# A gated two-layer network with experts on one core: the orders of three engines and the PSUM banks laid out anew

## Chip, core, metric

The kernel runs on one core of a Trainium2 chip. The metric is device microseconds of one execution, as the median of several runs.

## What is computed

The input is x, 4 x 256 tokens of 256 numbers (1024 tokens), and a context of the same shape. Four gated residual steps follow one another:

```python
x = x + tanh(g_xattn[0]) * wkv(w, u, layernorm(x), ctx)      # a scan along the sequence, exp and running max
x = x + tanh(g_ffn[0])   * quantised_ffn(layernorm(x))       # ternary weights, 8-bit rows, silu(gate) * up, 1024 inner
x = x + tanh(g_xattn[1]) * cross_attention(layernorm(x), ctx) # 32 heads of 8; q and k rms-normed; softmax
x = x + tanh(g_ffn[1])   * moe(layernorm(x))                 # 64 experts of 64 inner, top 8 of the logits, a shared one
```

In the quantised step a weight becomes round(w / mean|w|) cut to -1, 0, 1, and a row of tokens round(x / s) with s = max|x| / 127. In the expert step every expert is computed for all tokens, and its inner rows are multiplied by the token's routing weight, which is zero for experts that were not chosen:

```python
gu = einsum('nh,eih->nei', x, gu_w); inter = silu(gu[..., :I]) * gu[..., I:]
out = einsum('nei,ehi->nh', inter * W[:, :, None], dp_w) + sigmoid(x @ g1.T) * shared(x)
```

## The kernel before

The kernel is written in raw instructions: five engines with a program each, semaphores between them, and the order of the work written out by hand. TensorE (PE) has the matrix products and transposes, VectorE (DVE) and ScalarE (ACT) share the elementwise work and empty PSUM, SyncE (SP) issues all the DMAs. Each engine's program is a list of calls of small functions, and the three lists are meant to match: `turn_norm(q, b0)` on PE transposes the rows of the q-th layernorm into bank b0, `high_halves(q, b0)` on ACT and `low_halves(q, b0)` on DVE read them there. Where a name has two arguments, the last is the PSUM bank (of eight). A bank is taken by PE only when its former reader is done, so bank numbers set waits too.

The 1024 tokens are eight tiles of 128, in two halves of 512. Products that need more than 16-bit precision are made of a high and a low f16 part (three products for one). Twelve norms in all (`NORM_TILES`, L290) are computed in an order given by the list `FORMER`; `stats(q)` gathers mean and variance, `norm(q)` (L986 to L989, L1028) waits for ACT's root (`norm_root`, L564, L566), and from norm 8 on the root is made on DVE itself.

There are three parts.

The front (to the first expert product): the scan, the quantised step for tokens of the first half, attention for that half (`scores`, ACT's `probabilities`, `weighted_values`, DVE's `heads_sum` and `heads_out`), the router's `logits` (L1690), and the first expert weights. For the quantised step ACT scales each of the three weights to integers (`to_integers`, L584) and cuts one from below (`clamp_from_below`, L590), DVE makes them ternary (`ternary_weights`, L1109, L1110, L1113); ACT scales the tokens' rows (`tokens_to_integers`, L667); PE multiplies (`gate_product`, `up_product`, four matmuls of 128x512 a tile, L1602); ACT takes the SiLU of the gate's (`ffn_silu`, L688), and DVE multiplies by the up product (`ffn_inner`, L1206). `project` and `turn_rows` prepare keys and queries (ACT evicts them at L629, L632, L634), `row_sums` and `rows` rms-norm them on DVE (three Newton steps of three instructions each for 64 numbers, L1000 to L1002, among them).

The first half's experts: 65 chunks follow one another. Chunks 0 to 31 are the 32 pairs of experts for the first 512 tokens, chunk 32 the shared expert, chunks 33 to 64 the pairs for the second half. A chunk is, on PE, two products into PSUM (gate and up; `experts_in`, L1562, six matmuls each) and, two chunks later, one out of the inner rows into the accumulators in banks 0, 1, 4 and 5 (`experts_out`, L1892, six matmuls); on ACT the SiLU (`experts_silu`, L931 to L934) and a high part (`experts_high`, L941); on DVE the product with the up half (L1478, L1481), the low part (`experts_low`, L1472) and the routing weight (L1491, L1494). The weights of a pair come from memory in f32 into one of two staging slots (`load_entry`, L499 to L510) and are split by ACT (`weights_high`, L732) and DVE (`weights_low`, L1277) into one of nine weight slots; SP issues the load of the next entry only when both halves of the last but one are done. Entries are numbered by pair.

Beside chunks 0 to 27 runs the second half's share of all the rest: its quantised step (in halves of a tile, `wide_products`, `wide_silu`, `wide_inner`), its norms 8 to 11, its attention and its logits. Three tables say what stands where: `BESIDE_SCALAR` (L319), `BESIDE_VECTOR` and `BESIDE_PRODUCTS`, by chunk and place. PE's loop is: first product of chunk c, what stands at (c, "A"), second product, (c, "B"), the output of chunk c - 2, (c, "C"). DVE's is: product of c, A, low part of c - 1, B, weighting of c, C. ACT's is: SiLU of c, A, high part of c - 1, B. The gate and up products have one pair of banks in the first half, and `gate_bank` gives a second pair only after the shared chunk. From chunk 28 on nothing but experts is left on PE.

Of the kernel before, what the change touches and what calls it, by code (L numbers as in the profile page):

```python
# [16 lines left out]
B, S, D = 4, 256, 256  # L17
# [29 lines left out]
def bass_flamingo(nc, x_in, ctxT_in, wkv_in, g_in, ffn_in, proj_in, gate_in, gu_in, dp_in,  # L47
                  identf_in, identh_in, routing, out):
    with ExitStack() as stack:
# [260 lines left out]
        def of_keys(n):  # L310
# [10 lines left out]
                ("turned_rows", 9, 7), ("wide_silu", 5, 1, 4)],  # L321
            (1, "A"): [("ffn_turned", 4, 6), ("ffn_scale", 5), ("wide_silu", 6, 0, 6), ("wide_silu", 6, 1, 4)],
            (2, "A"): [("weights_high", 5), ("ffn_turned", 5, 6), ("ffn_scale", 6), ("wide_silu", 7, 0, 6),
                ("weights_high", 6), ("wide_silu", 7, 1, 4)],
            (3, "A"): [("weights_high", 7), ("ffn_turned", 6, 4), ("ffn_scale", 7)],
            (4, "A"): [("ffn_turned", 7, 4)],
            (4, "B"): [("high_halves", 8, 4), ("weights_high", 8)],
            (5, "B"): [("project", 10, 7), ("project", 11, 6), ("weights_high", 9), ("project", 12, 7),
                ("project", 13, 6), ("weights_high", 10)],
            (6, "B"): [("split", 10), ("split", 11), ("high_halves", 9, 4)],  # L330
            (7, "B"): [("project", 14, 7), ("project", 15, 6)],
            (8, "A"): [("weights_high", 11)],
            (9, "A"): [("turned_rows", 10, 7), ("turned_rows", 11, 6), ("weights_high", 12)],
            (9, "B"): [("split", 12), ("split", 13)],
            (10, "A"): [("weights_high", 13)],
            (10, "B"): [("table_exp_tanh",), ("probabilities", 32, 4), ("probabilities", 33, 6)],
            (11, "A"): [("probabilities", 34, 4), ("probabilities", 35, 6)],
            (11, "B"): [("weights_high", 14), ("turned_rows", 12, 4), ("turned_rows", 13, 6)],
            (12, "A"): [("probabilities", 36, 4)],
            (12, "B"): [("probabilities", 37, 6), ("probabilities", 38, 4), ("weights_high", 15),  # L340
                ("probabilities", 39, 6)],
            (13, "B"): [("weights_high", 16), ("probabilities", 40, 4), ("split", 14), ("probabilities", 41, 6)],
            (14, "A"): [("probabilities", 42, 4)],
            (14, "B"): [("weights_high", 17), ("probabilities", 43, 4), ("probabilities", 44, 6),
                ("weights_high", 18), ("probabilities", 45, 4)],
            (15, "B"): [("split", 15), ("weights_high", 19), ("probabilities", 46, 6), ("weights_high", 20)],
            (16, "A"): [("probabilities", 47, 6), ("turned_rows", 14, 5)],
            (16, "B"): [("weights_high", 21), ("turned_rows", 15, 6), ("weights_high", 22)],
            (17, "B"): [("weights_high", 23), ("probabilities", 48, 4), ("probabilities", 49, 6)],
            (18, "A"): [("probabilities", 50, 4), ("probabilities", 51, 6)],  # L350
            (18, "B"): [("weights_high", 24), ("probabilities", 52, 4)],
            (19, "A"): [("probabilities", 53, 6)],
            (19, "B"): [("probabilities", 54, 4), ("probabilities", 55, 6)],
            (20, "A"): [("weights_high", 25)],
            (20, "B"): [("probabilities", 56, 4), ("probabilities", 57, 6), ("probabilities", 58, 4),
                ("probabilities", 59, 6)],
            (21, "A"): [("weights_high", 26)],
            (21, "B"): [("probabilities", 60, 4), ("weights_high", 27), ("probabilities", 61, 6),
                ("probabilities", 62, 4)],
            (22, "B"): [("probabilities", 63, 4), ("table_silu",), ("high_halves", 10, 6), ("weights_high", 28),  # L360
                ("weights_high", 29)],
            (24, "A"): [("high_halves", 11, 4)],
            (25, "B"): [("table_exp_tanh",), ("weights_high", 30), ("exp_logits", 1), ("weights_high", 31)],
            (26, "A"): [("table_silu",)],
            (26, "B"): [("turned_weights", 1, 7)],
            (27, "B"): [("weights_high", 32)],
# [3 lines left out]
            (1, "A"): [("wide_inner", 6, 0, 7), ("wide_inner", 6, 1, 5)],  # L370
            (1, "B"): [("ffn_residual", 4, 4)],
            (2, "A"): [("weights_low", 5), ("wide_inner", 7, 0, 7), ("wide_inner", 7, 1, 5)],
            (2, "B"): [("ffn_residual", 5, 6), ("stats", 8)],
            (3, "A"): [("norm", 8)],
            (3, "C"): [("ffn_residual", 6, 7), ("weights_low", 6)],
            (4, "C"): [("ffn_residual", 7, 7), ("stats", 9), ("low_halves", 8, 4), ("weights_low", 7),
# [170 lines left out]
        def _(act):  # L547
# [21 lines left out]
            def norm_root(q):  # L569
                first_root(NORM_TILES[q][1] - NORM_TILES[q][0])  # L570
# [1404 lines left out]
```

## Time and profile before

| | us |
|---|---|
| runs | 498.81, 496.13, 495.12 |
| median | 496.13 |
| the profiled execution's own time | 494.66 |
| its span in the profile | 492.9 |
| its mean granted clock of PE | 0.946 |

The span runs from the first to the last instruction that the profile shows, and is 1.8 us shorter than the execution's own time. All that the prediction works out is read from this one execution, in microseconds from the start of its span. L562 and such are lines of the kernel before.

### The profile page before, as it was taken

What the parts mean: (1) busy time and instruction counts of PE and PEld (TensorE: products, weight loads), DVE (VectorE), ACT (ScalarE), POOL (GpSimd) and SP (SyncE); (2) the same over time, 40 slices, a digit from 0 to 9 for tenths busy, and PEclk for the clock granted to TensorE, in tenths of its full rate; (3) what the DMA queues carried; (4) which work ended last, traced back from release to release, by engine and by line L of the source; (5) the groups of instructions that cost most, each with busy time, mean ns of one, the idle gap of its engine ahead of it and who ended that gap; (6) DMA issues with size and microseconds to landing.
All of it is one profiled execution on the core that took longest, in us unless ns stands there. A gap on an engine that the chain in (4) does not pass through costs nothing.

```text
span 492.9 us, 7899 instructions
## 1 busy us (share of the span) xinstructions
PE 401.6 (81%) x2606; PEld 191.7 (39%) x2606; DVE 384.4 (78%) x867; ACT 305.9 (62%) x473; POOL 0.2 (0%) x4
## 2 busy tenths in 40 slices
PE   1041765777774999989999899899999999999994
PEld 1020353332332555444334433444444444444442
DVE  5999489898999789999878876886546776677744
ACT  5989576689893785648887678463233445544431
POOL 0000000000000000000000000000000000000000
PEclk9996889595998799999999999999999999999999
DMA  8420000000020151525246332234421755555501
GB/s 306 198 65 1 0 1 1 1 1 2 1 65 4 47 165 57 158 88 168 67 118 191 98 108 72 91 108 125 132 65 54 217 164 164 164 177 172 171 22 43
DMA packets 31491, 47.47 MB, mean 96 GB/s; under 512 B 5594, under 2 KB 15194, under 8 KB 30940
## 3 DMA queue, kind: packets, MB, share of 16 engines
q1 hardware_dynamic: 31452, 46.98, 30.4%
q8 instruction: 21, 0.34, 0.3%
q14 instruction: 18, 0.15, 0.1%
HBM read 45.65 MB, written 1.31 MB: 95 GB/s over the span
## 4 chain that ended last, share of the span: by engine, by line
PE 47%; DVE 30%; ACT 8%; issue 7%; DMA 5%; SPq 2%; DVEq 0%; ACTq 0%
PE ps L1562 25%; PE ps L1892 12%; PE ps L1667 4%; DMA regP<-in_dp_dram 4%; PE ps L1655 2%; DVE regW L1277 2%; DVE bn L1009 1%; DVE tiny L1194 1%; ACT regO L584 1%; DVE xn L1028 1%; DVE regW L1481 1%; DVE regW L1472 1%; PE ps L1583 1%; DVE rep L1155 1%; DMA regC<-in_ctxT_dram 1%
## 5 line engine op out<-in xcount | busy, mean ns | idle before, releaser
L1562 PE MATMUL ps<-hH,regC 128*128 128x512 f16 x264 | 85.5, 379 | 1.1 <-ACT regW L934 0.9
L1481 DVE TENSOR_TENSOR regW<-ps,regW 128x512 f32<-128x512 f32 x65 | 44.9, 690 | 52.6 <-PE ps L1562 50.1
L934 ACT ACTIVATE regW<-ps 128x512 f32<-128x512 f32 x52 | 31.0, 596 | 86.6 <-PE ps L1562 83.5
L1562 PE MATMUL ps<-hH,regW 128*128 128x512 f16 x248 | 81.8, 386 | 1.4 <-ACT regW L934 0.8
L1562 PE MATMUL ps<-hL,regC 128*128 128x512 f16 x132 | 50.0, 379 | 0.0
L1892 PE MATMUL ps<-regW,regC 128*128 128x512 f16 x198 | 48.2, 379 | 0.5 <-DVE regW L1472 0.5
L1562 PE MATMUL ps<-hL,regW 128*128 128x512 f16 x124 | 47.8, 385 | 0.0
L1892 PE MATMUL ps<-regW 128*128 128x512 f16 x186 | 45.3, 380 | 0.7 <-DVE regW L1472 0.7
L1472 DVE TENSOR_TENSOR regW<-regW 128x512 f16<-128x512 f32 x65 | 44.4, 682 | 1.0 <-ACT regW L941 0.7
L941 ACT CAST regW<-regW 128x512 f16<-128x512 f32 x65 | 39.8, 612 | 6.4 <-DVE regW L1494 6.1
L1562 PEld LDWEIGHTS ps<-hH,regC 128*128 128x128 f16 x264 | 25.8, 98 | 33.3 <-issue 2.6
L723 ACT ACTIVATE exs<-ps 128x1024 f32<-128x1024 f32 x32 | 32.0, 1023 | 9.4 <-PE ps L1655 8.6
L1562 PEld LDWEIGHTS ps<-hH,regW 128*128 128x128 f16 x248 | 24.5, 99 | 33.0 <-issue 3.9
L1494 DVE TENSOR_TENSOR regW<-regW 128x512 f32<-128x512 f32 x52 | 35.6, 685 | 0.1
L723 ACT ACTIVATE regF<-ps 128x1024 f32<-128x1024 f32 x32 | 32.0, 1026 | 5.0 <-PE ps L1667 2.2
L732 ACT ACTIVATE regC<-regP 128x768 f16<-128x768 f32 x30 | 25.3, 844 | 15.7 <-DMA regP<-in_dp_dram 15.7
L1277 DVE SCALAR_TENSOR_TENSOR regC<-regP,regC 128x768 f16<-128x768 f32 x30 | 28.5, 953 | 8.1 <-ACT regC L732 8.0
L1554 PE MATMUL ps<-identf,xn 128*128 128x128 f32 x64 | 12.6, 341 | 26.4 <-DVE xn L1028 15.8
L1655 PE MATMUL ps<-regO,KT 32*128 32x256 f16 x256 | 21.8, 290 | 9.4 <-ACT exs L723 3.8
L1892 PEld LDWEIGHTS ps<-regW,regC 128*128 128x128 f16 x198 | 19.1, 98 | 24.1 <-DVE regW L1472 1.0
L732 ACT ACTIVATE regW<-regP 128x768 f16<-128x768 f32 x27 | 22.6, 844 | 8.8 <-DMA regP<-in_dp_dram 8.5
L1277 DVE SCALAR_TENSOR_TENSOR regW<-regP,regW 128x768 f16<-128x768 f32 x27 | 25.5, 952 | 2.9 <-ACT regW L732 2.9
(189 smaller groups left out, 657.1 us busy)
## 6 DMA issues: line engine op xcount, KB each, us to landing
regW<-routing_dram SPq DMA_DIRECT2D x130, 128.0 KB, 3.1
regP<-in_gu_dram SPq DMA_DIRECT2D x56, 256.0 KB, 2.7
regP<-in_dp_dram SPq DMA_DIRECT2D x56, 128.0 KB, 2.8
regO<-in_ffn_dram SPq DMA_DIRECT2D x3, 1024.0 KB, 9.0
x<-in_x_dram SPq DMA_DIRECT2D x2, 512.0 KB, 8.2
regC<-in_ctxT_dram SPq DMA_DIRECT2D x1, 1024.0 KB, 5.0
out_dram<-x SPq DMA_DIRECT2D x2, 512.0 KB, 3.3
regP<-in_proj_dram SPq DMA_DIRECT2D x1, 768.0 KB, 12.1
```

The lines of the kernel that those rows point to most:

```text
L723: nc.scalar.activation(Ex[u % NE], bank(b0, 2).rearrange("p (j n) -> p j n", j=2), ACT.Exp, scale=float(HD) ** -0.5).then_inc(prob_ready, 1)
L732: nc.scalar.activation(mwH[e % NW], mst[:, e % NS, :], ACT.Copy, scale=W_SCALE).then_inc(mwH_ready, 1)
L934: nc.scalar.activation(sgm[:, c % 2, :], bank(gate_bank(c)), ACT.Silu, scale=UNSCALE).then_inc(esilu_done, 1)
L941: nc.scalar.copy(inH[:, d % 2, :], inter[:, d % 2, :]).then_inc(inH_ready, 1)
L1277: V.scalar_tensor_tensor(mwL[e % NW], mst[:, e % NS, :], W_SCALE, mwH[e % NW], ALU.mult, ALU.subtract).then_inc(mwL_ready, 1)
L1472: V.tensor_tensor(inL[:, d % 2, :], inter[:, d % 2, :], inH[:, d % 2, :], ALU.subtract).then_inc(inL_ready, 1)
L1481: V.tensor_tensor(rows, bank(gate_bank(c) + 1), rows, ALU.mult).then_inc(et_done, 1)
L1494: V.tensor_tensor(rows, route[:, c % NR, :], sgm[:, c % 2, :], ALU.mult).then_inc(inter_ready, 1)
L1562: mm = T.matmul(out_ap, w(k), a(k), start=(n == 0), stop=(n == 3 * DK - 1))
L1655: mm = T.matmul(bank(b0 + jj)[:, mt * S:(mt + 1) * S], KT[r:r + 32, g, b * S + mt * P:b * S + (mt + 1) * P], QT[r:r + 32, g, (b % 2) * S:( ...
L1667: mm = T.matmul(bank(bk)[32 * j:32 * j + HD + 1, 0:S], vaug[:, 2 * b + mt, 4 * g + j, :], Ex[u % NE][:, j % 2, mt * S:(mt + 1) * S], start ...
L1892: mm = T.matmul(bank(ACC[h] + k), w[s][:, at], a[:, c % 2, :], start=(c == 0 and n == 0), stop=(c == NCH - 1 and n == 2), skip_group_check ...
```

## The change

Each engine's list of calls is put in another order, and PSUM's bank numbers with it. It touches the lists of the front on ACT, DVE and PE, and the three tables beside the first half's experts. Each engine makes the same calls with the same shapes as before; SP's order, the chunks and their loop, the buffers, and all from chunk 28 on stay. The diff is cut to the lines that the prediction speaks of; of a table one or two lines stand. The functions' bodies are nine lines higher up in the kernel after (L1562 before is L1553 after).

```diff
         BESIDE_SCALAR = {
...
-            (4, "B"): [("high_halves", 8, 4), ("weights_high", 8)],
...
+            (5, "A"): [("high_halves", 8, 6)],
...
         BESIDE_VECTOR = {
...
-            (5, "C"): [("row_sums", 10), ("row_sums", 11), ("rows", 5), ("norm", 9)],
...
+            (12, "C"): [("norm", 9)],
+            (13, "C"): [("low_halves", 9, 6), ("heads_sum", 18, 5), ("weights_low", 19), ("heads_sum", 19, 4),
+                ("rows", 6)],
...
         BESIDE_PRODUCTS = {
...
-            (1, "A"): [("turn_rows", 9, 7), ("wide_products", 5, 1, 4)],
+            (1, "A"): [("wide_products", 5, 1, 4), ("turn_rows", 9, 7)],
...
-            (25, "A"): [("logits", 1, 7)],
```

DVE's list in the front, its beginning and its end:

```diff
             sums_a(0)
             sums_b(0)
+            sums_c(0)
             sums_a(1)
             sums_b(1)
-            sums_c(0)
+            sums_c(1)
             low_part(1)
             low_part(2)
-            sums_c(1)
+            weight_scales()
             quotient(0)
             quotient(1)
-            weight_scales()
-            row_sums(0)
+            ternary_weights(0)
             add_y(0, 4)
             stats(1)
-            ternary_weights(0)
+            ternary_weights(1)
+            row_sums(0)
+            row_sums(1)
+            ternary_weights(2)
             norm(1)
             token_scales(0)
-            ternary_weights(1)
-            ternary_weights(2)
-            ffn_inner(0, 4)
+            ffn_inner(0, 6)
...
+            weights_low(4)
             norm(7)
-            weights_low(2)
-            weights_low(3)
             low_halves(7, 2)
             logits(0, 1)
-            weights_low(4)
```

PE's list in the front, its beginning:

```diff
             turn_norm(0, 4)
-            project(0, 7)
-            project(1, 6)
             sum_weights()
+            project(0, 6)
+            project(1, 7)
             turn_y(0, 4)
-            turn_norm(1, 6)
-            up_product(0, 4)
-            gate_product(0, 6)
+            turn_norm(1, 2)
+            gate_product(0, 4)
+            up_product(0, 6)
             gate_product(1, 2)
```

In the tables these calls move too. The weights' entries 13, 14, 15, 16, 17, 19, 30, 31 and 32 are split on DVE at (10, "A"), 11C, 12C, 13B, 14C, 15B, 26B, 26C and 27C before, and at 8C, 9B, 10B, 11C, 11C, 13C, 25A, 26A and 27A now. `turn_rows(9)` changes places with the wide product beside it in 1A; norm 9, its low halves, `project(14)` and `project(15)`, two `rows` and `ffn_residual(7)` move from chunks 4 to 10 to chunks 11 to 16; norm 10 moves from 18A to 17C and norm 11 from 22C to 23C; the second half's logits move on PE from 25A to 25C.

The first place is ACT between the scan's exponentials and the quantised products, before norm 1's root (L564, L566 before, L555, L557 after). Before:

```order
L629 ACTIVATE kc<-ps 128x256
L632 ACTIVATE sq<-ps 128x256
L634 ACTIVATE vaug<-ps 128x32x8
L629 ACTIVATE kc<-ps 128x256
L632 ACTIVATE sq<-ps 128x256
L634 ACTIVATE vaug<-ps 128x32x8
L584 ACTIVATE regO<-regO,magic,rws 128x2048 x3
L564 ACTIVATE lnv<-ve 128x4
L566 ACTIVATE root<-lnv 128x4
L758 ACT_TABLE_LOAD
L590 ACTIVATE fw<-regO,magic 128x2048
```

After:

```order
L575 ACTIVATE regO<-regO,magic,rws 128x2048
L620 ACTIVATE kc<-ps 128x256
L623 ACTIVATE sq<-ps 128x256
L625 ACTIVATE vaug<-ps 128x32x8
L575 ACTIVATE regO<-regO,magic,rws 128x2048
L620 ACTIVATE kc<-ps 128x256
L623 ACTIVATE sq<-ps 128x256
L625 ACTIVATE vaug<-ps 128x32x8
L581 ACTIVATE fw<-regO,magic 128x2048
L575 ACTIVATE regO<-regO,magic,rws 128x2048
L555 ACTIVATE lnv<-ve 128x4
L557 ACTIVATE root<-lnv 128x4
```

The three scalings of weights (regO) stand apart now, with the evictions of two projections (kc, sq, vaug) between them, and the clamp (fw) stands ahead of the root instead of behind it.

The second place is DVE at the end of the front, from the last norm's statistics (bn, mv) to the logits (regF, 128x4x65). Before:

```order
L1009 BN_STATS bn<-x 128x6 x2
L1012 BN_AGGR mv<-bn 128x2 x2
L977 TENSOR_SCALAR ve<-mv 128x2
L986 TENSOR_TENSOR newt<-ve,root 128x2
L987 TENSOR_TENSOR newt<-newt,root 128x2
L988 TENSOR_SCALAR newt<-newt 128x2
L989 TENSOR_TENSOR rstd<-newt,root 128x2
L1028 TENSOR_SCALAR xn<-x,mv,rstd 128x256 x2
L1277 SCALAR_TENSOR_TENSOR regW<-regP,regW 128x768 x2
L1170 TENSOR_TENSOR hL<-ps,hH 128x256 x2
L1250 TENSOR_SCALAR regF<-ps 128x4x65
```

After:

```order
L1000 BN_STATS bn<-x 128x6 x2
L1003 BN_AGGR mv<-bn 128x2 x2
L968 TENSOR_SCALAR ve<-mv 128x2
L1268 SCALAR_TENSOR_TENSOR regC<-regP,regC 128x768
L977 TENSOR_TENSOR newt<-ve,root 128x2
L978 TENSOR_TENSOR newt<-newt,root 128x2
L979 TENSOR_SCALAR newt<-newt 128x2
L980 TENSOR_TENSOR rstd<-newt,root 128x2
L1019 TENSOR_SCALAR xn<-x,mv,rstd 128x256 x2
L1161 TENSOR_TENSOR hL<-ps,hH 128x256 x2
L1241 TENSOR_SCALAR regF<-ps 128x4x65
```

The two low splits of expert weights (regW) between the norm's rows (xn) and the low halves (hL) are gone from here, and another one (regC) stands between the statistics and the root's steps.

The third place is PE where the rows of norm 9 are turned (L1554 before, in chunk 6; L1545 after, in chunk 13). Before:

```order
L1892 MATMUL ps<-regW,regC 128x512 x6
L1554 MATMUL ps<-identf,xn 128x128 x4
L1562 MATMUL ps<-hH,regC 128x512
L1562 MATMUL ps<-hL,regC 128x512
L1562 MATMUL ps<-hH,regC 128x512 x2
L1562 MATMUL ps<-hL,regC 128x512
L1562 MATMUL ps<-hH,regC 128x512 x2
L1562 MATMUL ps<-hL,regC 128x512
```

After:

```order
L1883 MATMUL ps<-regW 128x512 x6
L1545 MATMUL ps<-identf,xn 128x128 x4
L1658 MATMUL ps<-exs,vaug 9x256 x8
L1658 MATMUL ps<-regF,vaug 9x256 x8
L1553 MATMUL ps<-projH,hH 128x256
L1553 MATMUL ps<-projL,hH 128x256
L1553 MATMUL ps<-projH,hL 128x256
L1553 MATMUL ps<-projH,hH 128x256
```

Before, the next expert product (hH, hL) stood behind the turned rows; now two weighted values (exs and regF with vaug) and then the projection of these very rows (projH, projL) stand there.

## Rows read from the trace of the kernel before

**Rows 1.** The page's busy time, share of the span and instructions of each engine.

```profile
PE 401.6 (81%) x2606; PEld 191.7 (39%) x2606; DVE 384.4 (78%) x867; ACT 305.9 (62%) x473; POOL 0.2 (0%) x4
```

**Rows 2.** Stretches: length, busy PE, PEld, DVE, ACT, POOL (instructions), PE's clock, DMA share, GB/s.

```profile
0.00:162.34 162.34, 85.91 (x743) 46.33 (x744) 139.11 (x355) 120.74 (x187) 0.20 (x4) 0.86 0.14 51
162.34:230.43 68.09, 64.39 (x367) 33.71 (x364) 62.72 (x170) 47.64 (x81) 0.00 (x0) 0.97 0.36 107
230.43:277.24 46.81, 45.44 (x368) 19.15 (x367) 37.61 (x71) 38.16 (x49) 0.00 (x0) 1.00 0.42 127
277.24:341.31 64.07, 60.48 (x443) 26.61 (x441) 49.20 (x128) 38.88 (x58) 0.00 (x0) 1.00 0.32 100
```

**Rows 3.** Chain of waits from 341.31 us: start, us, what.

```profile
345.37 2.59 PE ps L1562 x12
347.96 1.29 PE ps L1892 x6
```

**Rows 4.** DVE's waits, 56 to 162 us: for whom, us in total, times, longest.

```profile
DVE regF L1206 <- ACT regF L688: 6.1, 1, 6.1
DVE regO L1163 <- PE ps L1583: 1.1, 3, 0.7
DVE newt L986 <- ACT root L566: 1.1, 2, 0.6
```

**Rows 5.** PE's waits in the first half's experts, 162.4 to 341.4 us.

```profile
PE ps L1554 <- DVE xn L1028: 1.9, 2, 1.5
PE ps L1562 <- ACT regW L934: 1.7, 2, 0.9
PE ps L1655 <- DVE x L1243: 1.4, 2, 1.0
PE ps L1644 <- DVE x L1226: 1.0, 1, 1.0
PE ps L1562 <- DVE regW L1481: 0.7, 2, 0.6
```

**Rows 6.** ACT's timeline, 33 to 50 us: start, us, instruction [idle before, releaser].

```profile
33.36 0.39 ACT L629 ACTIVATE kc<-ps 128x256 f32<-128x256 f32 x1 [0.64 <-PE ps L1562]
...
36.35 6.06 ACT L584 ACTIVATE regO<-regO,magic,rws 128x2048 f32<-128x2048 f32 x3 [0.63 <-DVE rws L1103]
...
47.00 2.08 ACT L667 ACTIVATE xn<-xn,magic,rqs 128x256 f32<-128x256 f32 x4 [0.94 <-DVE rqs L1190]
```

**Rows 7.** DVE's timeline, 42 to 57 us.

```profile
42.85 0.16 DVE L986 TENSOR_TENSOR newt<-ve,root 128x4 f32<-128x4 f32 x1 [0.55 <-ACT root L566]
...
47.53 1.22 DVE L1109 TENSOR_SCALAR fw<-regO 128x2048 bf16<-128x2048 f32 x1
48.78 0.69 DVE L1110 TENSOR_SCALAR fw<-fw 128x2048 bf16<-128x2048 bf16 x1
55.62 1.28 DVE L1206 SCALAR_TENSOR_TENSOR regF<-ps,sus,regF 128x1024 f32<-128x1024 f32 x1 [6.14 <-ACT regF L688]
```

**Rows 8.** Chain of waits at the first quantised products.

```profile
51.22 3.22 PE ps L1602 x8
```

**Rows 9.** Two stretches around them, columns as in rows 2.

```profile
51.20:54.40 3.20, 3.18 (x9) 1.20 (x10) 0.00 (x0) 0.00 (x0) 0.00 (x0) 0.57 0.00 0
54.40:58.00 3.60, 3.48 (x17) 1.37 (x14) 2.35 (x2) 3.12 (x3) 0.00 (x0) 1.00 0.00 0
```

**Rows 10.** Timelines of DVE and ACT at the front's end.

```profile
157.97 1.82 DVE L1277 SCALAR_TENSOR_TENSOR regW<-regP,regW 128x768 f16<-128x768 f32 x2
...
159.01 0.65 ACT L661 CAST hH<-ps 128x256 f16<-128x256 f32 x2 [0.97 <-PE ps L1554]
```

**Rows 11.** DVE's groups by form, all the span: us busy, mean ns, idle before.

```profile
L1277 DVE SCALAR_TENSOR_TENSOR regC<-regP,regC 128x768 f16<-128x768 f32 x30 | 28.5, 953 | 8.1 <-ACT regC L732 8.0
...
L1000 DVE SCALAR_TENSOR_TENSOR newt<-rstd,ve 128x64 f32<-128x64 f32 x12 | 2.7, 225 | 0.4
```

**Rows 12.** Chain of waits from 296 us: a weight load behind its issue.

```profile
298.94 4.28 DMA regP<-in_dp_dram
```

More of the change, by code:

```diff
@@ new lines, in bass_flamingo @@
+            (3, "C"): [("narrow", 6, 5)],
+            (5, "A"): [("turn_norm", 8, 6)],
+            (5, "C"): [("turn_hidden", 7, 4), ("project", 10, 7), ("project", 11, 6)],
+            (6, "A"): [("project", 12, 7), ("project", 13, 6)],
+            (7, "B"): [("turn_rows", 10, 7)],
+            (8, "A"): [("turn_rows", 11, 7)],
+            (8, "C"): [("scores", 32, 4), ("scores", 33, 6)],
+            (11, "B"): [("scores", 34, 4)],
+            (12, "A"): [("scores", 35, 4), ("weighted_values", 16, 7), ("narrow", 7, 6)],
@@ L469, in bass_flamingo @@
+            (21, "B"): [("scores", 61, 4), ("scores", 62, 6)],
+            (21, "C"): [("scores", 63, 4)],
+            (22, "A"): [("weighted_values", 30, 7), ("weighted_values", 31, 6)],
+            (22, "B"): [("heads_out", 6, 4), ("heads_out", 7, 6)],
+            (25, "A"): [("turn_norm", 11, 4)],
+            (25, "C"): [("logits", 1, 7)],
+            (27, "B"): [("turn_weights", 1, 7)],
         }
@@ L1761, in _ @@
[L1761 to L1772 removed]
+            turn_hidden(2, 4)
+            narrow(2, 7)
+            turn_norm(2, 4)
+            turn_hidden(3, 2)
+            project(2, 6)
@@ new lines, in _ @@
+            project(3, 5)
+            project(4, 4)
+            narrow(3, 6)
+            project(5, 5)
+            turn_rows(0, 3)
+            turn_rows(1, 4)
+            turn_norm(3, 4)
+            turn_rows(2, 3)
+            turn_rows(3, 2)
+            scores(0, 0)
+            scores(1, 4)
+            scores(2, 6)
+            scores(3, 2)
+            scores(4, 0)
+            scores(5, 4)
+            weighted_values(0, 7)
+            scores(6, 2)
+            weighted_values(1, 6)
@@ new lines, in _ @@
+            turn_norm(4, 6)
+            scores(7, 0)
+            scores(8, 4)
+            weighted_values(2, 3)
+            weighted_values(3, 2)
+            scores(9, 0)
+            scores(10, 4)
+            scores(11, 6)
+            project(6, 3)
+            project(7, 1)
+            scores(12, 4)
+            weighted_values(4, 2)
+            weighted_values(5, 7)
+            turn_rows(4, 6)
+            turn_rows(5, 3)
+            scores(13, 0)
+            scores(14, 6)
+            scores(15, 4)
@@ L1798, in _ @@
-            scores(31, 4)
-            weighted_values(14, 2)
-            weighted_values(15, 3)
-            turn_norm(6, 4)
+            scores(20, 0)
+            scores(21, 6)
+            weighted_values(8, 3)
+            turn_y(1, 4)
+            weighted_values(9, 2)
+            turn_norm(5, 0)
+            weighted_values(10, 7)
+            scores(22, 4)
+            scores(23, 2)
+            scores(24, 6)
+            scores(25, 4)
+            scores(26, 2)
+            weighted_values(11, 1)
@@ L1802, in _ @@
+            scores(27, 6)
+            weighted_values(12, 5)
+            scores(28, 2)
+            scores(29, 6)
+            scores(30, 0)
+            weighted_values(13, 5)
+            scores(31, 2)
+            weighted_values(14, 4)
+            weighted_values(15, 7)
+            turn_norm(6, 5)
             heads_out(2, 2)
-            heads_out(3, 6)
+            heads_out(3, 0)
             wide_products(4, 0, 4)
```

550 lines of the change are left out of this document (234 added, 316 removed).

## The prediction

> **What bounds the kernel now.** I read the page's busy line first, then the busy times by stage, then each engine's waits inside a stage, and last the instructions around the waits. The busy line puts TensorE (PE) at 81% [rows 1]. That mean hides four stages [rows 2]. In the front (0 to 162.34 us, before the first expert product) VectorE (DVE) is busy 139.1 of 162.3 us and PE only 85.9: DVE bounds it. In the first half's experts PE is busy 64.39 + 45.44 + 60.48 = 170.3 of 179.0 us (chunks 0 to 10, 11 to 17, 18 to 28), while DVE is busy 92% of the first of these stretches (62.72 of 68.09) and 80% of the second. From 341.31 us on, the start of chunk 29, the chain of waits is a plain beat of PE: 2.59 us into an expert pair and 1.29 out of it, 3.88 us a chunk [rows 3]. The change leaves that part alone, so the question is how late PE arrives at it.
>
> What is there to win? In the front, after 56 us, DVE waits 6.1 us for the first SiLU, and the next largest group is 1.1 us [rows 4]. An order can't do away with work, so the front has few us to give. In the first half PE is idle 8.7 us, most of it behind DVE: 1.9 us for a norm's rows and 1.4 + 1.0 us for residuals, with 1.7 us for the experts' SiLU [rows 5]. The 8.7 us are the largest gain that the loop can have.
>
> **Part 1, the quantised products.** Before, ScalarE (ACT) runs the three scalings to integers in one piece (6.06 us from 36.35), 2.0 each, then the root for norm 1, then the clamp, as large as a scaling, beside DVE's norm [rows 6]. Now the scalings can start when the weight scales are there, after DVE's low parts (32.0, the 3.87 us of quotients no longer ahead), but two projections' evictions (three instructions of 0.39 us each [rows 6], 1.0 us a set) and the clamp stand before the root. 32.6 + 6.06 + 2 x 1.0 + 2.0 = 42.7: the root is as early as before (DVE took it up at 42.85 [rows 7]). DVE, though, now also has the last step of the second ternary weight (0.69), one row sum (0.4) and the third ternary weight (1.22 + 0.69 [rows 7]) ahead of norm 1; these lay in its 6.1 us gap. 3.0 us of work less the 0.6 us wait for the root [rows 4]: norm 1 begins near 45.4, and the tokens' integers at 49.5 instead of 47.00 [rows 6], 2.5 us later. Part comes back, since the gate product of tile 0 is now first and its SiLU runs beside the up product. 53.75 (51.22 + 2.5) + 3.22 for 8 products [rows 8] = 57.0, so `ffn_inner(0)` comes at 57.2 instead of 55.62 [rows 7]: + 1.6 us. Tile 1's up product is still the sixth call: 24 products, 3.22 + 16 x 0.205 (3.48 / 17 [rows 9]) = 6.5, and a bank's wait let it through near 61.0, where DVE is ready at 60.2: + 0.8. One row sum, and what followed it, is done already: - 0.6. Together + 1.8 us (bounds 0.5, if the clock is up when the burst starts, and 4.8, if it stays down throughout).
>
> The clock is the unsure part. From 51.2 to 54.4 us the granted clock was 0.57, so mostly the 1.2 GHz level, and 1.00 just after [rows 9]; my sum takes the first 8 products at that level again.
> The Trainium skill (TensorE: Matmul & The Clock Gate, What's actually happening) says that the throttled state is the default and activity releases it; by that the burst starts slow wherever it is put, and the sum stays + 1.8, or turns into rival C if release comes later. The trace agrees as to the start (0.57), and can't show the new place.
>
> **Part 2, the front's middle.** Between 67 and 90 us DVE's calls are mixed anew (row sums, residuals and turned rows stand behind one another), so the 1.1 us of waits for turned rows [rows 4] get other work beside them: - 0.9 us (bounds 0 and - 1.5).
>
> **Part 3, the front's end.** Before, two low splits of expert weights (1.82 us) filled the time between DVE's last norm and its low halves, while PE turned the rows and ACT made the high halves (begun 159.01, 0.65 us) [rows 10]. Now these two stand far earlier and a third (0.95 us [rows 11]) goes before the norm's roots. That one hides the 0.6 us wait for the root [rows 4] and costs some 0.4 us, and the low halves wait uncovered: the norm's rows end where the splits began, 157.97, and the high halves at 159.66, 1.6 us of nothing on DVE, while the two splits' 1.82 us now lie in busy time. 1.3 us of that shows before the first expert product, by my order of the calls ahead of it, and 0.4 + 1.3 less 0.4 for waits that the early splits fill is + 1.3 us (bounds 0 and 2.3). Front: 1.8 - 0.9 + 1.3 = + 2.2 us, so the first expert product starts near 164.5.
>
> **Part 4, chunks 0 to 10.** Counting calls in both orders, by chunk 10 DVE loses one statistics, one norm, two `rows` (each twelve chained steps at 0.225 us [rows 11], 2.7 us, and five more, some 3.8 by estimate), one low halves, two row sums, two low splits of rows and a residual, and gains two weight splits (0.95 each): about 14 us less. PE loses 2.7 us of work beside the experts. DVE held PE here, so its waits on a norm (1.9), on a residual (1.0) and on DVE's expert product (0.6) go [rows 5]; 1.0 us of new ones comes (`wide_products(5, 1)` stands ahead of the turned rows and waits for its bank, and `turn_norm(8)` is close behind its norm). - 2.7 - 3.5 + 1.0 = - 5.2, say - 5.0 us (bounds 0 and - 6.5).
>
> **Part 5, chunks 11 to 17.** The 14 us land here, and norm 10 (3.2 us) out of chunk 18. DVE's load is then 37.6 + 14 + 3.2 = 54.8 us, some 3 less where neighbouring instructions overlap; PE's is 45.4 + 2.7 = 48 in a stretch that took 46.8 [rows 2]. PE runs ahead of DVE by a chunk at most, since one pair of gate banks holds the products. Waits that I find one by one: 0.7 at the first scores behind their probabilities (chunk 12), 2.8 in chunk 13 (`turn_norm(9)` right behind norm 9; `project(14)` behind low halves 9), 1.4 in 15 and 16. Weights are a part of it: ACT waits for entry 19 before high halves 9, and a weight load took 4.28 us from issue to landing [rows 12]. Part 5: 2.7 + 4.9 - 1.4 (old waits of scores on a residual [rows 5]) = + 6.2 us (bounds + 2.7, if DVE's backlog hides in PE's lead, and + 12).
> The Trainium skill (DMA: Bandwidth & Descriptors, Anatomy of one DMA) gives, for the descriptor path of GpSimd, 2.0 us fixed and bytes at 436 GB/s: by it such a load of 128 KB would be an estimated 2.3 us and the sum 2 us less. Here the loads are on SyncE's hardware queue and share it, and the trace's 4.28 us [rows 12] decides.
>
> **Part 6, chunks 18 to 28.** Most of the old waits that lie here go, some 2.9 of the 8.7 us (entries 30 to 32 are split earlier). New: 1.2 in 18 and 19 (low halves 10 and heads' sums), 0.3 in 22, and 1.9 in 26, whose experts' product waits behind the logits, one place later. Together about - 0.6 us (bounds - 3 and + 3).
>
> **The sum.** 2.2 - 5.0 + 6.2 - 0.6 = + 2.8 us on the profiled execution's 494.66: 497.5. The median of the runs before (496.13) lies 1.5 us above that execution, so the forecast for a median is 498.9 us.
>
> **The rivals.** (A) The evening-out works. For it: DVE at 92% in one stretch and 80% in the next is uneven, the order moves 14 us across that line, and nearly all of PE's 8.7 us are behind something that an order can move. Against: the front. If all goes and nothing comes: 496.13 + 2.2 - 8.7 = 489.6. (B) Slower, by one mechanism: in chunks 11 to 17 DVE becomes the bound. It decides from the point where DVE's product of chunk 13 comes after PE has done both of that chunk's products. Then the stretch takes DVE's 54.8 us for PE's 46.8, + 8.0, and DVE, which is late, splits three entries late, each 1.3 us more: + 12.0 in place of + 6.2, so 504.7. For it: the sum of loads. Against: neighbouring DVE instructions overlap. (C) PE's clock: the burst's 24 products all run at 0.40 us, 9.6 us in place of 6.5, + 3.0: 501.9.
>
> **How the numbers follow.** About 1% is what a measurement of this kernel tells from no change: 491.2 and 501.1. My forecast (496 to 501): 0.50. A: 0.18. B: 0.20. C: 0.12. So faster 0.18, same 0.50, slower 0.32. The range is 491.5 to 505.5: below it lies most of A, above it the worse half of B's tail, some 2 in 10 together.
>
> **What would show it.** The first expert product starts at 164 to 165 us; DVE's gap before `ffn_inner(0)` is 7 to 8 us instead of 6.1. PE's idle time up to chunk 10 is about 1 us. DVE is over 93% busy in chunks 11 to 17, and PE waits there for DVE. PE begins chunk 29 some 2 to 4 us later than 341.31. I am wrong if the first expert product starts before 162 us (parts 1 to 3), if PE is idle under 6 us over the first half (part 5), or if the beat from chunk 29 on isn't 3.88 us.

## The result, and the profile after

| | before | after |
|---|---|---|
| median of 20 runs, us | 495.54 | 498.46 |
| lowest to highest | 494.04 to 498.81 | 495.64 to 501.4 |
| profiled execution, us | 494.66 | 498.54 |
| its span | 492.9 | 496.8 |
| its mean granted clock of PE | 0.946 | 0.938 |

The ratio of after to before is 1.0047, with a 95% interval of 1.003 to 1.0064: slower by 1.5 to 3.2 us, real, and inside the 1% that the prediction called no change. The quotient of the two medians is 1.0059; here and below it lies inside the interval, up to 0.0024 from the ratio. The forecast was 498.9.

The stretches of the kernel after, cut at the same places of the program as in [rows 2] (first expert product, start of chunk 11, of chunk 18, of chunk 29), with the same columns:

```profile
0.00:164.45 164.45, 90.44 (x743) 48.12 (x743) 139.58 (x356) 121.18 (x187) 0.20 (x4) 0.84 0.14 51
164.45:230.18 65.73, 61.84 (x342) 32.27 (x340) 53.93 (x133) 43.59 (x71) 0.00 (x0) 0.96 0.39 121
230.18:282.11 51.93, 47.64 (x391) 21.57 (x390) 46.51 (x112) 38.59 (x54) 0.00 (x0) 1.00 0.31 94
282.11:345.22 63.11, 60.04 (x447) 26.86 (x444) 49.76 (x126) 41.86 (x61) 0.00 (x0) 1.00 0.37 114
```

The lengths against [rows 2] are + 2.11, - 2.36, + 5.12 and - 0.96 us, + 3.91 in all, and the executions' own times differ by 3.88. From chunk 29 on the beat is the same 3.88 us.

DVE's timeline in the front answers to [rows 7]:

```profile
45.22 0.16 DVE L977 TENSOR_TENSOR newt<-ve,root 128x4 f32<-128x4 f32 x1
...
57.14 1.28 DVE L1197 SCALAR_TENSOR_TENSOR regF<-ps,sus,regF 128x1024 f32<-128x1024 f32 x1 [7.81 <-PE ps L1593]
...
60.59 1.28 DVE L1197 SCALAR_TENSOR_TENSOR regF<-ps,sus,exs 128x1024 f32<-128x1024 f32 x1 [0.47 <-PE ps L1593]
...
161.82 0.76 DVE L1161 TENSOR_TENSOR hL<-ps,hH 128x256 f16<-128x256 f32 x2 [1.41 <-ACT hH L652]
```

Norm 1's root steps begin at 45.22 instead of 42.85, `ffn_inner(0)` comes 1.52 us later than before, and the low halves at the front's end stand uncovered for 1.41 us. PE's waits answer to [rows 5]. From the first expert product to chunk 11:

```profile
PE ps L1593 <- ACT regF L703: 2.1, 1, 2.1
PE ps L1690 <- DVE Wf L1262: 1.0, 1, 1.0
PE ps L1646 <- ACT regO L645: 0.6, 1, 0.6
```

And in chunks 11 to 17:

```profile
PE ps L1553 <- DVE hL L1161: 1.4, 1, 1.4
PE ps L1646 <- ACT exs L714: 1.2, 1, 1.2
PE ps L1658 <- ACT regF L714: 0.7, 1, 0.7
PE ps L1646 <- ACT regF L714: 0.5, 1, 0.5
PE ps L1553 <- DVE regW L1472: 0.4, 1, 0.4
```

None of the old waits of the first group is left (a norm's rows, a residual, DVE's product). Others of the same size stand in their place, and most name ACT, not DVE. The largest, 2.1 us, is a wide product that waits for a bank which `ffn_turned(5)` (L703) frees. A wait of the same kind was in this stretch before, with 0.6 us (L712 and L1602 before are L703 and L1593 after):

```profile
PE ps L1602 <- ACT regF L712: 0.6, 1, 0.6
```

The chain of waits in chunks 2 and 3 tells what held ACT:

```profile
178.01 0.60 SPq L531
...
178.71 0.53 SPq L500
...
179.28 4.41 DMA regP<-in_dp_dram
...
184.46 1.10 ACT regF L703
...
185.70 1.19 PE ps L1593 x4
```

and ACT's timeline shows it standing:

```profile
180.61 0.85 ACT L723 ACTIVATE regC<-regP 128x768 f16<-128x768 f32 x1
183.71 0.84 ACT L723 ACTIVATE regC<-regP 128x768 f16<-128x768 f32 x1 [2.25 <-DMA regP<-in_dp_dram]
184.46 1.10 ACT L703 ACTIVATE regF<-ps,magic 128x1024 bf16<-128x1024 f32 x1
```

ACT's list now has the split of entry 6 (the second L723) right ahead of `ffn_turned(5)`. The entry's load is issued at 178.71, behind SyncE's route loads, and lands 4.4 us later. ACT takes its list in order, so the tile behind the split waits for a load that it doesn't need. Before, this split came after three other calls and waited for nothing:

```profile
182.38 0.83 ACT L732 ACTIVATE regC<-regP 128x768 f16<-128x768 f32 x1
```

Two further places look alike: a split of entry 12 ahead of `turned_rows(11)` (ACT waits 2.12 us, PE 0.6), and one of entry 19 ahead of `high_halves(9)` (ACT waits 1.29 us, DVE 0.47 for those high halves, and PE 1.4 for the low ones).

### The profile page after: what moved, and what is told of

Same layout as the page of the kernel before. It is cut to its first block, busy times and chain, and to the rows that moved or that the text cites. A ratio compares the mean times of both kernels' runs of the same rounds, so it can differ in the third digit from the quotient of the medians.

```text
span 496.8 us, 7898 instructions
## 1 busy us (share of the span) xinstructions
PE 405.3 (82%) x2606; PEld 194.7 (39%) x2606; DVE 384.2 (77%) x867; ACT 305.3 (61%) x473; POOL 0.2 (0%) x4
## 4 chain that ended last, share of the span: by engine, by line
PE 46%; DVE 32%; issue 7%; DMA 6%; ACT 5%; SPq 4%; DVEq 0%; ACTq 0%
PE ps L1553 25%; PE ps L1883 12%; DMA regP<-in_dp_dram 5%; SPq L531 2%; PE ps L1658 2%; DVE bn L1000 2%; PE ps L1593 2%; DVE xn L1019 1%; DVE regO L1226 1%; PE ps L1646 1%; DVE regW L1463 1%; DVE regW L1268 1%; DMA regC<-in_ctxT_dram 1%; DVE regW L1485 1%; DVE tiny L1185 1%
## 5 line engine op out<-in xcount | busy, mean ns | idle before, releaser
L1553 PE MATMUL ps<-hH,regC 128*128 128x512 f16 x264 | 85.5, 379 | 0.4 <-DVE regW L1472 0.4
L1553 PE MATMUL ps<-hH,regW 128*128 128x512 f16 x248 | 81.2, 384 | 1.2 <-DVE regW L1472 1.2
L1553 PE MATMUL ps<-hL,regC 128*128 128x512 f16 x132 | 50.0, 379 | 0.0
L1553 PE MATMUL ps<-hL,regW 128*128 128x512 f16 x124 | 47.5, 383 | 0.0
L1553 PEld LDWEIGHTS ps<-hH,regC 128*128 128x128 f16 x264 | 25.8, 98 | 32.2 <-issue 2.1
L1545 PE MATMUL ps<-identf,xn 128*128 128x128 f32 x64 | 13.4, 361 | 30.1 <-DVE xn L1019 14.0
L1553 PEld LDWEIGHTS ps<-hH,regW 128*128 128x128 f16 x248 | 24.6, 99 | 32.9 <-issue 3.4
L723 ACT ACTIVATE regC<-regP 128x768 f16<-128x768 f32 x30 | 25.3, 844 | 8.7 <-DMA regP<-in_dp_dram 8.2
L723 ACT ACTIVATE regW<-regP 128x768 f16<-128x768 f32 x27 | 22.7, 844 | 12.5 <-DMA regP<-in_dp_dram 12.3
```

Of the source, the lines that this page charges most:

```text
L723: nc.scalar.activation(mwH[e % NW], mst[:, e % NS, :], ACT.Copy, scale=W_SCALE).then_inc(mwH_ready, 1)
L1545: mm = T.transpose(bank(b0 + k)[:, (t - a) * P:(t - a + 1) * P], xn[:, t, k * P:(k + 1) * P], identf[:, :])
L1553: mm = T.matmul(out_ap, w(k), a(k), start=(n == 0), stop=(n == 3 * DK - 1))
```

## The experiments

In each run's text "after" is the changed kernel. Medians of different runs of the kernel before went from 495.5 to 497.0, so ratios are compared, and a difference in us is a difference of two ratios times the median of before. Positions come from one profiled execution each, and that one isn't always near the median of its run: e_norm's is the shortest of its twelve (495.00), e_end's the longest (497.99).

**The two halves of the change.** The run m_front has the new lists of the front with the old three tables, m_loop the reverse.

> The new order of the front alone, the first half's experts by the tables of before. Theory (the front costs about 2 us and the loop adds about 1 to 2): first expert product near 164.5 us, median 1.8 to 2.5 us over before (about 497.6). Rival (the front's delay is absorbed by waits in the loop, all of the loss is the loop's): first product late all the same, but the median within 0.7 us of before. A fault of the measurement (one execution was slow) would put the first product at 162 to 163.

Measured: median 499.45 beside 496.62, ratio 1.0033 (1.0006 to 1.0059): + 1.6 us. The first expert product is at 166.47, 2 us later than expected.

> The new tables beside the first half's experts alone, with the front of before. Theory (the loop's new order gives nothing: chunks 0 to 10 win 2.4 us, 11 to 17 lose 5.1, 18 to 28 win 1): median 0.5 to 2 us over before (about 496.5 to 497.5), first product at 162.3. Rival (the loop's order is better by itself and suffers only from a late start): median 1 us or more under before.

Measured: 497.05 beside 496.62, ratio 1.0005 (0.9977 to 1.0032): + 0.2 us. The first product came at 165.48 here, with the very front that gave 162.34 in the profile of before. Of these 3.14 us, 0.80 are there when PE turns norm 1's rows (48.54 instead of 47.74), 0.36 more at `ffn_inner(0)`, and 1.98 come between the fourth `ffn_inner` and the first product. PE's clock differs too. Its timeline at the quantised products, before and then in m_loop:

```profile
51.22 6.66 PE L1602 MATMUL ps<-fw,regF 128*128 128x512 bf16 x24 [1.40 <-issue]
```

```profile
48.54 2.08 PE L1545 MATMUL ps<-identf,xn 128*128 128x128 f32 x8 [11.27 <-ACT xn L658]
52.02 9.32 PE L1593 MATMUL ps<-fw,regF 128*128 128x512 bf16 x31 [1.40 <-issue]
```

At full clock such a product takes 0.222 us (28 in 6.21 us in e_warm below), so 24 would take 5.3 us and 31 would take 6.9: the low clock cost PE 1.3 us in one execution and 2.4 in the other. Behind the fourth `ffn_inner` the mean granted clock is 0.83 before and 0.81 here. That the clock makes all of the 3.14 us isn't shown.

Front alone and tables alone give + 1.6 and + 0.2, together + 1.8, and the whole change + 2.3 us (0.0047). By these ratios the loss is the front's, and the tables win and lose about the same; the two intervals overlap, so the profiles are asked too. Four have the old front (before, m_loop, e_oldfront, b_small), with the fourth `ffn_inner` at 64.67 to 66.27 us (mean 65.7) and the first product at 162.34 to 165.48 (163.4). Five have the new one unchanged (after, m_front, e_loads, e_first, e_small), at 66.63 to 68.50 (67.5) and 164.45 to 167.69 (166.0). The new front is late by 1.8 us at the first place and by 2.6 at the second.

**Norm 1 first.** In the kernel after:

```diff
             ternary_weights(0)
             add_y(0, 4)
             stats(1)
-            ternary_weights(1)
             row_sums(0)
-            row_sums(1)
-            ternary_weights(2)
             norm(1)
             token_scales(0)
+            ternary_weights(1)
+            row_sums(1)
+            ternary_weights(2)
```

> The kernel after, with one row sum, and the last two ternary steps behind DVE's norm 1 and token scales instead of ahead of them. Theory of part 1 (DVE's 3 us of work ahead of norm 1 make ffn_inner(0) late): norm 1 about 2.3 us earlier (limited by ACT's root, at 43.5), tokens' integers near 47.3, ffn_inner(0) near 55.0 instead of 57.14, first expert product near 162.5 and the median 1.5 to 2 us under the kernel after (about 496.7). Rival (the PE clock or the two ternary weights, now later, bound the products): ffn_inner(0) not before 56.5 and the median within 0.7 us of after.

Measured: 498.27, ratio 1.0022 (0.9993 to 1.0051), some 1.2 us under after's 1.0047, with overlapping intervals. DVE's timeline:

```profile
44.65 1.38 DVE L1019 TENSOR_SCALAR xn<-x,mv,rstd 128x256 f32<-128x256 f32 x4
...
55.91 1.28 DVE L1197 SCALAR_TENSOR_TENSOR regF<-ps,sus,regF 128x1024 f32<-128x1024 f32 x1 [5.10 <-PE ps L1593]
...
59.95 1.28 DVE L1197 SCALAR_TENSOR_TENSOR regF<-ps,sus,exs 128x1024 f32<-128x1024 f32 x1 [1.06 <-PE ps L1593]
```

Norm 1's rows begin 1.36 us earlier (44.65 instead of 46.01), not 2.3: ACT's root is the limit. `ffn_inner(0)` gains 1.23 us and the second tile 0.64: it waits 1.06 us for its products, 27 of which take 8.45 us here, most of it at the low clock. The mechanism is there, at half the size. What it is worth at the end is less sure: e_both below lies 1.6 us under e_loads, again with overlapping intervals.

**Splits of weights behind the urgent call.** In the kernel after, ACT's table:

```diff
-            (2, "A"): [("weights_high", 5), ("weights_high", 6), ("ffn_turned", 5, 4), ("ffn_scale", 6)],
+            (2, "A"): [("weights_high", 5), ("ffn_turned", 5, 4), ("ffn_scale", 6), ("weights_high", 6)],
-            (7, "B"): [("weights_high", 11), ("weights_high", 12), ("turned_rows", 11, 7)],
+            (7, "B"): [("weights_high", 11), ("turned_rows", 11, 7), ("weights_high", 12)],
-            (13, "B"): [("probabilities", 39, 4), ("weights_high", 19), ("high_halves", 9, 6), ("project", 14, 7),
+            (13, "B"): [("probabilities", 39, 4), ("high_halves", 9, 6), ("weights_high", 19), ("project", 14, 7),
```

> The kernel after, with three splits of expert weights on ACT (entries 6, 12, 19) put behind the call that PE waits for (ffn_turned 5, turned_rows 11, high_halves 9) instead of ahead of it. Theory W (ACT stands still before a split until its load lands, 2.25, 2.12 and 1.29 us, and PE waits 2.1, 0.6 and 1.4 us behind it): these three waits of PE go, PE's chunk 29 starts 2 to 4 us earlier than 345.22, median 495 to 496.5. Rival D (DVE is the bound in chunks 11 to 17, 46.5 of 51.9 us busy, and takes up what ACT gives back): the waits turn into waits on DVE, the median is within 1 us of the kernel after.

Measured: 495.19, ratio 0.9959 (0.9937 to 0.9982), clear of after's 1.0047 and 4.4 us under it. PE takes 175.2 us from the first expert product to chunk 29, 180.8 in after, so DVE doesn't take up what ACT gives back (theory W held, rival D didn't). The run e_first has the first of the three moves alone:

> The kernel after, with only one of the three moves of the run e_loads: the split of entry 6 on ACT stands behind ffn_scale 6 instead of ahead of ffn_turned 5 (chunk 2). Theory W1 (this one wait, 2.25 us on ACT and 2.1 on PE, makes most of the 3.3 us): the start of PE's chunk 3 is 2 us nearer to the first product than in the kernel after (20.7 to 21.9 us behind it in place of 23.95) and the median 2 us under after (about 496.5). Rival W3 (the gain came from the split of entry 19 in chunk 13, or from all three together): median less than 1 us under after.

Measured: 495.95, ratio 0.9984 (0.9954 to 1.0013), 3.1 us under after. The start of chunk 3 stands 20.74 us behind the first product in both, 23.95 in after, and 22.7 to 25.4 in the other runs with the split ahead: a wait for a load comes out differently each time. In e_first PE still waits 3.3 us in chunk 13, where the third move leaves 0.7 in e_loads:

```profile
PE ps L1553 <- DVE hL L1161: 3.3, 1, 3.3
```

W1 holds: the place of this one call is worth 3.1 us, clear of noise, more than the whole loss of 2.3. The 1.2 us from e_first to e_loads are inside the noise, and no run moves the splits of entries 12 and 19 one at a time; the waits point to entry 19.

**Smaller loads.** Each load from entry 5 on moves a quarter of its bytes; the rest of the expert weights in the slot is old data, so this part isn't computed from the inputs. The run e_small does this to the kernel after, b_small to the kernel before.

```diff
-                sp.dma_start(mst[:, e % NS, 0:2 * DK * P], gu_in[:, p, :]).then_inc(ld_pair[e % NS], 16)
-                sp.dma_start(mst[:, e % NS, 2 * DK * P:PW], dp_in[:, p, :]).then_inc(ld_pair[e % NS], 16)
+                w = 1 if e < NS + EARLY else 4
+                n1, n2 = 2 * DK * P // w, D // w
+                sp.dma_start(mst[:, e % NS, 0:n1], gu_in[:, p, 0:n1]).then_inc(ld_pair[e % NS], 16)
+                sp.dma_start(mst[:, e % NS, 2 * DK * P:2 * DK * P + n2], dp_in[:, p, 0:n2]).then_inc(ld_pair[e % NS], 16)
```

> The kernel after, with only a quarter of the bytes of each weight load from entry 5 on (64 KB and 32 KB in place of 256 and 128 KB; the rest of the staging slot keeps old numbers, so this part of the expert weights is not computed from the inputs). Theory W (bytes in flight make ACT stand before its splits): ACT's idle time before its splits of weights falls from 21 us to under 8, the start of chunk 3 comes 20.7 us behind the first product in place of 23.95, median 3 us under after. Rival F (what ACT waits for is mostly the late issue: SyncE's route loads and the splits that free a slot): the loads shorten by some 1 us each and ACT's idle time falls by less than half, median 0 to 1.5 us under after.

> The control to e_small: the kernel before, with a quarter of the bytes of each weight load from entry 5 on (that part of the expert weights is not computed from the inputs). In the kernel after this took 6 us off the median. If waits for loads are what the new order of the experts' part added, the kernel before gains clearly less, 1 to 3 us (median 493.5 to 495.5). If every order of this kernel pays for the loads alike, it gains 5 to 6 us too (median near 491), and the loads explain nothing of the difference between the two kernels.

Measured: e_small 492.34, ratio 0.9903 (0.9879 to 0.9927); b_small 493.53, ratio 0.9934 (0.9913 to 0.9955). The kernel after gains 7.1 us by ratio, twice what was expected; the kernel before 3.3, a little over its 1 to 3. Chunk 3 starts 20.76 us behind the first product, as theory W said. ACT's groups of splits, in after and then in e_small:

```profile
L723 ACT ACTIVATE regC<-regP 128x768 f16<-128x768 f32 x30 | 25.3, 844 | 8.7 <-DMA regP<-in_dp_dram 8.2
L723 ACT ACTIVATE regW<-regP 128x768 f16<-128x768 f32 x27 | 22.7, 844 | 12.5 <-DMA regP<-in_dp_dram 12.3 <-ACT vaug L625 0.2
```

```profile
L725 ACT ACTIVATE regC<-regP 128x768 f16<-128x768 f32 x30 | 25.4, 846 | 3.6 <-DMA regP<-in_dp_dram 3.6
L725 ACT ACTIVATE regW<-regP 128x768 f16<-128x768 f32 x27 | 22.7, 845 | 5.4 <-DMA regP<-in_dp_dram 4.9 <-ACT vaug L627 0.4
```

ACT's idle time falls from 21.2 to 9.0 us. In the kernel before it was 24.5 us, more than in after, and yet cost less: what counts is who is queued behind the split. With small loads after is faster than before (0.9903 against 0.9934, intervals that overlap) although its front still costs 1.6 us. The new tables were thus worth some 2 to 3 us where loads are short: 1.5 + 1.6 by the ratios, and 2.0 by the profiles, where the stretch from the first expert product to chunk 29 takes 173.6 us in e_small and 175.6 in b_small. The load waits ate that. That it comes from the evening-out of DVE, and not from another part of the new tables, is argued and not shown.

**PE's clock.** In the kernel after, 32 extra matmuls (128x512 into bank 0, never read) ahead of `turn_norm(1, 2)` on PE and 6 behind it.

```diff
+            def warm(n):
+                for _ in range(n):
+                    T.matmul(bank(0), projH[:, 0, 0:P], ctxH[:, 0, 0:512], start=True, stop=True)
...
+            warm(32)
             turn_norm(1, 2)
+            warm(6)
             gate_product(0, 4)
```

> The kernel after, with 32 extra matmuls (128x512, their result in bank 0 is never read) ahead of PE's transposes for norm 1 and 6 behind them. Theory C (the burst of quantised products starts at the 1.2 GHz level because PE was idle 12 us before it): with PE busy ahead of it the granted clock is 1.0 from the first product, 8 products take 1.7 us in place of 3.3, ffn_inner(0) comes at 55.3 or earlier instead of 57.14 and ffn_inner(1) without its 0.5 to 1 us wait, median 1.5 to 2.5 us under after. Rival (the level doesn't follow what PE did just before, or the extra activity lowers the clock later): products still at 0.4 us each, or a lower clock in the stretch behind them, and the median within 0.7 us of after or above.

The stretches of after around the products (its transposes begin at 50.02, its products at 53.59), then those of e_warm, and PE's timeline at e_warm's products:

```profile
50.00:53.50 3.50, 2.17 (x8) 1.15 (x8) 0.00 (x0) 2.71 (x5) 0.00 (x0) 0.50 0.00 0
53.50:57.00 3.50, 3.41 (x9) 1.26 (x10) 0.00 (x0) 1.11 (x1) 0.00 (x0) 0.54 0.00 0
```

```profile
40.00:50.00 10.00, 4.81 (x23) 2.07 (x22) 8.82 (x28) 5.42 (x7) 0.00 (x0) 0.99 0.00 1
50.00:53.50 3.50, 3.50 (x13) 1.85 (x14) 0.00 (x0) 2.58 (x5) 0.00 (x0) 0.53 0.00 0
53.50:57.00 3.50, 3.50 (x18) 1.60 (x17) 0.87 (x1) 1.46 (x2) 0.00 (x0) 1.00 0.00 0
```

```profile
53.86 6.21 PE L1593 MATMUL ps<-fw,regF 128*128 128x512 bf16 x28
```

The 32 matmuls ended 5.2 us ahead of the transposes. The transposes and the six extra matmuls ran at the low level (0.53), in the products' stead. From the first product on the granted clock is 1.00 instead of 0.54 (2.4 GHz in place of mostly 1.2), 18 matmuls fit where 9 did, and `ffn_inner(0)` comes at 56.13 instead of 57.14 (55.3 was expected). The median is 497.92, ratio 1.0018 (0.9997 to 1.0039), some 1.4 us under after with overlapping intervals. That the level follows what PE did just before is shown; the gain of the median alone would not have shown it.
The Trainium skill (TensorE: Matmul & The Clock Gate, What's actually happening) says that the throttled state is the default and that activity releases the throttle. The traces agree: each of the runs without extra matmuls starts this burst at the low level, and only e_warm and e_all don't.

**The front's end.** In the kernel after, the splits of entries 2 and 3 go back behind norm 7 and that of entry 4 behind the logits, on DVE and on ACT, as in the kernel before. DVE's part:

```diff
             heads_sum(14, 4)
-            weights_low(2)
             heads_sum(15, 7)
             split_low(8)
             split_low(9)
-            weights_low(3)
...
-            weights_low(4)
             norm(7)
+            weights_low(2)
+            weights_low(3)
             low_halves(7, 2)
             logits(0, 1)
+            weights_low(4)
```

> The kernel after, with the splits of entries 2, 3 and 4 on ACT and DVE back where the kernel before has them at the end of the front (2 and 3 behind the last norm's root and rows, 4 behind the logits). Theory of part 3 (their early place costs 1.3 us ahead of the first product): first expert product 1 to 1.5 us earlier than in after (near 163.2), median 1 us under after. Rival (the early splits also load entries 5 and 6 earlier, or the work has only changed places): first product within 0.5 us of 164.45 or the gain lost again by chunk 3, where entries 5 and 6 would land later; median within 0.7 us of after or above.

Measured: 495.35, ratio 0.9969 (0.9945 to 0.9994), 3.9 us under after. The profiled execution shows less. Its first product is at 164.67, but its burst had run at the low clock and the fourth `ffn_inner` started 0.91 us later than in after (67.54 against 66.63), so the rest of the front is 0.7 us shorter, and chunk 3 stands 23.05 us behind the first product, 0.9 less than in after. These 1.6 us are located. Beside the five profiles with the new front, where the fourth `ffn_inner` and the first product are 97.8 to 99.2 us apart (mean 98.5), e_end's 97.1 is 1.4 less, which is what was expected of it. The profiled execution is also the longest of the run's twelve. Where the rest of the runs' 3.9 us comes from is open.

**Both mended, and more.** The run e_both is the kernel after with the edits of e_norm and e_loads; e_oldfront is m_loop with those of e_loads; e_all is e_both with the extra matmuls of e_warm.

> The kernel after with both edits, norm 1 ahead of the ternary weights on DVE and the three splits behind the urgent calls on ACT. If the parts add: 3.3 us and 0.2 to 1.5 us under after, median 493.7 to 495. Rival (the front's gain is lost in the burst's clock, as in e_norm): median as in e_loads, 495.2 within 0.5.

> The front of the kernel before, with the new tables and the three moved splits of e_loads. If the front of after costs 1.6 to 2 us (m_front): median 493.2 to 494 and under both kernels. If the front costs nothing when the loop's loads are out of the way: median 495 as in e_loads.

> All that helped: the kernel after with norm 1 ahead of the ternary weights, the three splits behind the urgent calls, and the extra matmuls that keep PE's clock up. If the clock's 1 us at ffn_inner(0) is worth anything at the end: median 0.5 to 1 us under e_both (492.37), so 491.4 to 491.9. If it is lost again in the front's middle, as e_warm suggested: 492.4 within 0.5.

Measured: e_both 492.37, ratio 0.9926 (0.9897 to 0.9954), under the 493.7 to 495 expected; e_oldfront 492.99, 0.9917 (0.9888 to 0.9946), 2.1 us under e_loads, which is the front's cost once more (intervals that just overlap); e_all 490.59, 0.9872 (0.9842 to 0.9902). In e_both the parts add: 6.0 us under after, where e_norm and e_loads have 1.2 and 4.4. e_all is 2.7 us under e_both (intervals that just touch), more than either expectation and than e_warm's 1.4. e_all beats the kernel before by 6.3 us and the kernel after by 8.7. In its products' stretch the clock is full:

```profile
53.00:56.00 3.00, 3.00 (x16) 1.36 (x14) 1.30 (x2) 1.87 (x2) 0.00 (x0) 1.00 0.00 0
```

`ffn_inner(0)` stands at 54.67 there, and the first product at 160.66.

## Why the prediction came out right

The forecast was 498.9 and the median 498.46, and both profiled executions differ by 3.88 us where the sum said 2.8. Step by step:

- **Part 1 (+ 1.8) held.** Norm 1 at 45.22 (forecast 45.4), `ffn_inner(0)` at 57.14 (57.2), the fourth tile 1.96 us later than before. The nine profiles with an old or a new front give 1.8 us for this place in the mean, so this isn't one lucky trace, and e_norm confirms that the work ahead of norm 1 is a cause. The 0.205 us for a product at full clock was low, 0.222 by e_warm.
- **Parts 2 and 3 (- 0.9 and + 1.3) held in sum only.** From the fourth `ffn_inner` on the front lost another 0.15 us where 0.4 was forecast; in the mean of the nine profiles it loses 0.9. The waits for turned rows are gone and the low halves wait 1.41 us (1.6 forecast). The early splits cost 1.4 us ahead of the first product by e_end's profile (1.3 forecast for part 3), but more at the end by its ratio, which one trace doesn't explain. The first product's 164.45 beside the forecast 164.5 is partly luck, since it moves by some us from one execution to the next. The runs' value for the whole front is + 1.6 (m_front) to + 2.1 us (e_loads against e_oldfront); the forecast was + 2.2.
- **Part 4 (- 5.0) was too large: - 2.36.** The step that failed is "1.0 us of new ones comes". PE's idle time in chunks 0 to 10 is 65.73 - 61.84 = 3.9 us, against 3.7 before. I had counted the new waits by who stands behind whom on DVE and PE, and missed the split ahead of `ffn_turned(5)` on ACT. The waits that were to go were also read too large for this stretch: of the norm's 1.9 us, 1.5 lie here. With the split of entry 6 moved (e_first) the stretch takes 61.65 us, - 6.4.
- **Part 5 (+ 6.2) was near: + 5.12.** 2.2 us of it are PE's moved work (2.7 forecast), 2.9 idle time (3.5 net forecast). The wait in chunk 13 is there, 1.4 us in after and 3.3 in e_first; DVE stands for the high halves behind the load of entry 19 for 0.5 and 2.5 us of it. Two of its steps failed. DVE's load didn't rise by 17 us but by 8.9 (37.61 to 46.51). Overlap of rows explains little of that: the durations of the stretch add up to 40.3 us before and 50.3 after, + 10.0. Most of it is that I had moved calls by their place in the tables, while DVE runs behind PE's chunks. `rows(7)`, in chunk 10 of the old table, ran behind PE's start of chunk 11 (230.43) already before, and norm 10's root and rows, in chunk 17 of the new one, run behind its start of chunk 18 (282.11); the first instruction of each, before and then after:

```profile
233.01 0.19 DVE L996 TENSOR_SCALAR ve<-ss 128x64 f32<-128x64 f32 x1
```

```profile
283.17 0.16 DVE L987 TENSOR_SCALAR ve<-mv 128x2 f32<-128x2 f32 x1
```

The second step that failed is DVE as the bound. DVE is 90% busy there, not over 93, and PE waits for ACT (2.4 us) at least as much as for DVE (1.8). Rival B's mechanism isn't what the runs show.
- **Part 6 (- 0.6) held: - 0.96**, though its list of waits didn't: 1.8 us behind probabilities and 1.2 behind DVE's product are there.
- **The sum** was 1.1 us short on the executions, and the step from execution to median (+ 1.5) came out at - 0.1 for after: two errors of opposite sign. That the forecast lies 0.4 us from the median is luck; it looks better than its working.
- **Rival A**, a gain from the new tables, was real: 2 to 3 us where loads are short, and with the three calls moved and the old front (e_oldfront) 4.1 us under before, of the 8.7 that it allowed. Rival C, the clock throughout the burst, didn't decide. It varies between executions: the burst's loss on PE, worked out in the same way, went from 1.3 us (before) to 2.9 (e_oldfront, 32 products in 9.98 us).

## What to carry to other kernels

On an engine that works in order, a call that waits for a transfer belongs behind the calls that others wait for, however early its data are wanted: one such pair in the wrong order cost 3 us here. When work is moved to even out two engines, read the third one's waits too, by what is queued behind each. The total idle time before a group of instructions says little: the kernel with more of it (24.5 us ahead of ACT's splits, 21.2 in after) was the faster one. Count moved work by when it runs in the trace, not by its place in a list.

## What the runs showed that was not expected

- A quarter of the bytes shortened a load's median from 2.9 to 2.2 us (256 to 64 KB), and took 7.1 us off the kernel after. How many of the loads were on the path isn't shown.
The Trainium skill (DMA: Bandwidth & Descriptors, Anatomy of one DMA) gives for GpSimd's path 2.0 us fixed and bytes at 436 GB/s, an estimated 2.15 and 2.6 us; on SyncE's queue the trace shows 2.2 and 2.9, near it, but 4.41 for the 128 KB that follow another load and the route loads.
- The same front put the first expert product at 162.34 and at 165.48 in two executions. A position in one trace of this kernel is good to 2 or 3 us only. A distance in which nothing waits for a load is good to 0.1 (20.73 to 20.76 from the first product to chunk 3, in six runs); with the wait in it, it went from 22.7 to 25.4.
- Work that computes nothing can pay: e_all, with 38 matmuls that nobody reads, is 2.7 us by ratio under e_both, and e_warm 1.4 under after. Neither difference is clear of noise by itself; the higher clock in the burst is.
